# Four self attentions: score blocks with two heads on the rows and two batches on the columns, without block-diagonal squares, and with the row scale applied to the products

## What is computed

```python
q = jnp.einsum('bsc,hcd->bhsd', xn, wq)
k = jnp.einsum('btc,hcd->bhtd', yn, wk)
v = jnp.einsum('btc,hcd->bhtd', yn, wv)
a = jax.nn.softmax(jnp.einsum('bhsd,bhtd->bhst', q, k) * D ** (-0.5), axis=-1)
if causal:
    a = a * mask
o = jnp.einsum('bhst,bhtd->bhsd', a, v)
```

| stage | sublayer | heads x depth | special |
|---|---|---|---|
| A | `l0_xattn`, part a1 | 16 x 32 | mask behind the softmax |
| B | `l0_attn` | 16 x 16 padded to 32, in 8 pairs | the second head of a pair is subtracted, weighted by lambda |
| C | `l3_attn` | 16 x 64 | the output overwrites `V` |
| D | `l3_ffn` | 8 x 32 | |

## Time and profile before

### The profile page before, as it was taken

How to read it: one execution, slowest core, us unless ns; L and a number is a source line. 1 busy time by engine, 2 the same in 40 slices (tenths; PEclk the granted TensorE clock), 3 DMA queues, 4 the chain that set the end, 5 groups by cost and what they waited for, 6 DMA issues and landing times. The chain is left out here.

```text
span 5024.1 us, 105344 instructions
## 1 busy us (share of the span) xinstructions
PE 4240.7 (84%) x42698; PEld 3189.1 (63%) x42698; DVE 2661.6 (53%) x5277; ACT 1804.4 (36%) x3793; POOL 712.2 (14%) x422
## 2 busy tenths in 40 slices
PE   5869999999874969999976679586899899997877
PEld 3649888889554856666632369442699666665465
DVE  5447777777245026555539822246333566664544
ACT  1225555555211324444523312120344344443111
POOL 0013222222001010000009610115122000001100
PEclk8789999999975989999988879798799999999985
DMA  1110000000011841111003268549111100000211
GB/s 59 38 32 17 17 17 20 21 17 1 30 49 63 317 152 46 51 42 42 16 25 86 70 265 302 205 146 119 51 43 40 34 22 22 29 16 36 70 42 34
DMA packets 185482, 339.59 MB, mean 68 GB/s; under 512 B 53379, under 2 KB 136660, under 8 KB 167156
## 3 DMA queue, kind: packets, MB, share of 16 engines
q1 hardware_dynamic: 175348, 318.88, 20.3%
q0 software_dynamic: 3072, 8.39, 0.5%
q10 hardware_dynamic: 6624, 6.03, 0.3%
HBM read 278.31 MB, written 31.60 MB: 62 GB/s over the span
## 5 line engine op out<-in xcount | busy, mean ns | idle before, releaser
L2691 DVE TENSOR_REDUCE block_max<-PS 128x1 f32<-128x512 f32 (+1 forms) x896 | 505.7, 627 | 299.8 <-PE PS L2551 299.0
L2640 ACT ACTIVATE probs_turned<-PS 128x512 f32<-128x512 f32 (+1 forms) x896 | 434.5, 571 | 562.4 <-PE PS L2572 562.3
L844 PE MATMUL PS<-context_turned,queries 128*128 128x512 f32 (+1 forms) x1536 | 362.3, 380 | 21.7 <-issue 17.0
L905 ACT CAST probs_turned<-PS 128x512 fp32r<-128x512 f32 (+1 forms) x512 | 232.2, 510 | 280.4 <-PE PS L856 280.4
L876 PE MATMUL PS<-probs_turned,context_part 128*128 128x256 f32 (+1 forms) x2496 | 330.7, 286 | 2.2 <-DVE weighted L953 2.2
L844 PEld LDWEIGHTS PS<-context_turned,queries 128*128 128x128 f32 x1536 | 274.3, 195 | 75.2 <-issue 20.5
L919 DVE TENSOR_TENSOR probs_turned<-PS,probs_turned 128x512 fp32r<-128x512 f32 (+1 forms) x512 | 276.6, 582 | 64.9 <-ACT probs_turned L905 62.9
L876 PEld LDWEIGHTS PS<-probs_turned,context_part 128*128 128x128 f32 (+1 forms) x2496 | 307.1, 189 | 2.4 <-DVE probs_turned L919 2.4
L2592 PEld LDWEIGHTS PS<-probs_turned,values 128*17 128x17 f32 x13312 | 191.5, 97 | 147.6 <-issue 120.9
L2551 PE MATMUL PS<-keys_turned,queries 32*128 32x512 f32 (+1 forms) x2048 | 241.2, 548 | 40.3 <-ACT probs_turned L2640 35.3
L911 ACT ACTIVATE probs<-PS,minus_max 128x1024 f32<-128x1024 f32 (+1 forms) x256 | 238.7, 933 | 81.8 <-DVE minus_max L964 80.7
(11 more groups left out here) (504 smaller groups left out, 7581.6 us busy)
## 6 DMA issues: line engine op xcount, KB each, us to landing
context_rows<-in_ctx SPq DMA_DIRECT2D x40, 768.0 KB
context_turned<-ctx_turned SPq DMA_DIRECT2D x32, 800.5 KB
routed_up<-in_L_ffn_W SPq DMA_DIRECT2D x23, 1024.0 KB, 7.6
routed_down<-in_L_ffn_W SPq DMA_DIRECT2D x23, 1024.0 KB, 5.0
routed_up<-in_L_ffn_wg_w SPq DMA_DIRECT2D x23, 1024.0 KB, 7.4
routed_second<-in_L_ffn_w_w SPq DMA_DIRECT2D x23, 1024.0 KB, 9.6
routed_down<-in_L_ffn_w_w SPq DMA_DIRECT2D x23, 1024.0 KB, 4.9
v_all<-v_turned SPq DMA_DIRECT2D x128, 128.0 KB, 20.4
```

Of the source, the lines that this page charges most:

```text
L844: last = nc.tensor.matmul(S[:, 512 * j:512 * j + cols], qs[a][:, v, p * P:(p + 1) * P], yT[b][:, v, 512 * j:512 * j + cols], start=(m == 0 ...
L2640: nc.scalar.activation(probs[0:kk, t % ring, i, 0:many].rearrange("p k c s -> p (k c s)"), PS[0:kk, bank_of("turned", t, i), 0:many * 2 * ...
L2691: nc.vector.tensor_reduce(part[:, b % 2, chunks[0]:chunks[-1] + 1, i, u // 2], bank, AX_X, ALU.max).then_inc(max_done.sem, 1)
```

## The change

`self_attention` is rewritten; nothing else in the program differs. What it does:

- TensorE and VectorE read `qT`, `kT` and `V` in place. The staging DMAs, their buffers and waits are gone.
- A score block holds two heads on the two halves of the rows (`x`) and the two batches on the columns (`y`). The number of score products is the same. Head group `g` now always goes to row half `g % 2` of the output, so that with `d = 32` four cells are in use, not eight.
- A 128-column block of `E` can be turned as it is, two heads by two batches: there are 8 transposes per tile in A, B and C and 4 in D. `squares`, its clearing and its two copies are gone.
- The products with V are 64 rows by 64 columns: 32 per tile in A, B and C, 16 in D, two records each. Batch `y` has its keys on rows `y*64` and its output on partitions `y*64`, so that two of the four 64 x 64 cells are in use. The order alternates between them, and between two banks.
- The probabilities are not scaled. The row sums go through four small products with halves of the identity (`sums`), and `take` multiplies the products with V by the reciprocals, in two instructions, one per bank. In B the addition of the two heads follows there.
- In A the mask is applied by GpSimd, in two halves, between the exponential and the transposes.
- `E`, the turned blocks and the row sums have two buffers, and the hardware loops are unrolled.

The core of the diff, left out where it only renames:

```diff
-                    for h in range(heads):
-                        g, k = h % groups, h // groups
-                        for b in range(2):
-                            last = nc.tensor.matmul(PS[b * SEQ:(b + 1) * SEQ, g, k * SEQ:(k + 1) * SEQ],
-                                                    qs[g * d:(g + 1) * d, u, k, b * SEQ:(b + 1) * SEQ],
-                                                    ks[g * d:(g + 1) * d, u, k, b * SEQ:(b + 1) * SEQ],
-                                                    start=True, stop=True)
+                    for j0 in range(0, pairs, groups):
+                        for turn in range(2):
+                            for y in range(2):
+                                for g in range(groups):
+                                    x = g % 2
+                                    j = j0 + (g // 2 + (groups // 2) * ((x + turn) % 2) if groups == 4 else (x + turn) % 2)
+                                    k = (2 * j + x) // groups
+                                    rows = slice(g * d, (g + 1) * d)
+                                    at = (j // groups) * P + y * SEQ
+                                    last = nc.tensor.matmul(PS[x * SEQ:(x + 1) * SEQ, j % groups, at:at + SEQ],
+                                                            qT[rows, k, tokens(i, y)], kT[rows, k, tokens(i, y)],
+                                                            start=True, stop=True)
...
-                    for pos in range(squares):
-                        h = head_of(pos)
-                        last = nc.tensor.matmul(O_ps[:, h * dv:(h + 1) * dv], turned_sb[:, pos, :],
-                                                vs[:, u, h * dv:(h + 1) * dv], start=True, stop=True)
+                def sums(i):
+
+                    pe.wait_ge(summed.sem, summed.at(i + 1))
+                    if i:
+
+                        pe.wait_ge(o_taken.sem, o_taken.at(2 * i))
+                    for x, y in ((0, 0), (0, 1), (1, 0), (1, 1)):
+                        out = PS[y * SEQ:(y + 1) * SEQ, sum_bank + x, sum_col:sum_col + pairs].rearrange("p (g k) -> p g k", k=deep)
+                        last = nc.tensor.matmul(out, core.ident[:, x * SEQ:(x + 1) * SEQ], total[:, i % 2, :, :, y], start=True, stop=True)
+                    last.then_inc(moved.sem, 1)
...
+                def output(i, f):
+                    pe.wait_ge(t_act.sem, t_act.at(i * tfills + f + 1))
+                    for j0 in range(f * per_fill, (f + 1) * per_fill, 2):
+                        for turn in range(2):
+                            for x in range(2):
+                                for y in range(2):
+                                    j = j0 + (y + turn) % 2
+                                    rows = slice(y * SEQ, (y + 1) * SEQ)
+                                    at = (j // 2 * 2 + x) * dv
+                                    h = j if diff else 2 * j + x
+                                    last = nc.tensor.matmul(PS[rows, o_bank + j % 2, at:at + dv], ET[rows, i % 2, j, x * SEQ:(x + 1) * SEQ],
+                                                            V[rows, i, h * dv:(h + 1) * dv], start=True, stop=True)
...
-                    then(nc.vector.reciprocal(total[:], total[:]))
-                    if diff:
-                        odd = total[:, 1::2, :]
-                        then(nc.vector.tensor_scalar(odd, odd, minus_lam, None, ALU.mult))
-                    then(nc.vector.tensor_tensor(E[:], E[:], total[:].unsqueeze(3).broadcast_to([P, groups, per, SEQ]),
-                                                 ALU.mult))
-                    if mask is not None:
-                        Ef = E[:].rearrange("p g k t -> p (g k) t")
-                        then(nc.vector.tensor_tensor(Ef, Ef, mask[:].unsqueeze(1).broadcast_to([P, heads, SEQ]), ALU.mult))
...
+                    nc.vector.reciprocal(inverse[:, u].rearrange("p (k g x) -> p x g k", g=groups, x=2),
+                                         PS[:, sum_bank:sum_bank + 2, sum_col:sum_col + pairs].rearrange("p x (g k) -> p x g k", k=deep)
+                                         ).then_inc(inverted.sem, 1)
...
+                        nc.vector.tensor_tensor(by_bank(to), PS[:, o_bank + b, 0:pairs * dv].rearrange("p (q x n) -> p q x n", x=2, n=dv),
+                                                scale_of.unsqueeze(3).broadcast_to([P, pairs // 2, 2, dv]), ALU.mult).then_inc(o_taken.sem, 1)
...
+                        for k in range(deep):
+                            nc.gpsimd.tensor_tensor(kept[:, i % 2, :, k], E[:, i % 2, :, k],
+                                                    mask[:].unsqueeze(1).unsqueeze(1).broadcast_to([P, groups, 2, SEQ]),
+                                                    ALU.mult).then_inc(masked.sem, 1)
```

More of the change, by code:

```diff
@@ L425, in self_attention @@
     nc, PS = core.nc, core.PS
-    qc = qT.shape[1]
     groups = P // d
-    per = heads // groups
+    pairs = heads // 2
+    deep = pairs // groups
+    per_fill = 4
+    tfills = pairs // per_fill
     diff = minus_lam is not None
[L430 to L433, removed]
+    t_bank, o_bank = 4, 6
+    sum_bank, sum_col = (2, 0) if d == 64 else (o_bank, 448)
@@ L438, in self_attention @@
[L438 to L443, removed]
-    with ExitStack() as own:
[L446 to L453, removed]
+    o_ready, o_taken = core.semaphore("out_ready"), core.semaphore("out_taken")
@@ L454, in self_attention, with over_keys @@
         warm = core.sb(own, "warm", [1, 1])
[L455 to L458, removed]
+        S = PS[:, 0:groups, 0:deep * P].rearrange("p g (k y t) -> p g k y t", y=2, t=SEQ)
+        def over_keys(x):
+            return x.unsqueeze(4).broadcast_to([P, groups, deep, 2, SEQ])
         with nc.Block() as block:
[L460 to L480, removed]
@@ L502, in output @@
[L502 to L514, removed]
-                    for pos in range(squares):
-                        h = head_of(pos)
-                        last = nc.tensor.matmul(O_ps[:, h * dv:(h + 1) * dv], turned_sb[:, pos, :],
-                                                vs[:, u, h * dv:(h + 1) * dv], start=True, stop=True)
-                    last.then_inc(o_ready.sem, 1)
@@ new lines, in turn_exps @@
+                def turn_exps(i, f):
+                    n = i * tfills + f
+                    if mask is None:
+                        pe.wait_ge(exps.sem, exps.at(i + 1))
+                    else:
+                        pe.wait_ge(masked.sem, masked.at(i * deep + (f + 1) * deep // tfills))
+                    if n >= 2:
+                        pe.wait_ge(t_act.sem, t_act.at(n - 1))
+                    for m in range(per_fill):
+                        j = f * per_fill + m
+                        last = nc.tensor.transpose(PS[:, t_bank + n % 2, m * P:(m + 1) * P],
+                                                   kept[:, i % 2, j % groups, j // groups].rearrange("p y t -> p (y t)"), core.ident[:])
+                    last.then_inc(turned.sem, 1)
@@ L532, in _ @@
+                scores(0)
+                for i in range(TILES):
+                    if i + 1 < TILES:
+                        scores(i + 1)
+                    for f in range(tfills):
+                        turn_exps(i, f)
+                    sums(i)
+                    for f in range(tfills):
+                        output(i, f)
             @block.vector
@@ L605, in self_attention @@
-    probs.passed(2 * TILES)
-    if d == 64:
-        begun.passed(TILES)
+    o_taken.passed(2 * TILES)
     turned.passed(tfills * TILES)
-    t_act.passed(tfills * TILES + 2)
-    step.passed(steps * TILES + 1)
+    t_act.passed(tfills * TILES)
+    if diff:
+        signed.passed(TILES)
+        scaled.passed(TILES)
+    if mask is not None:
+        masked.passed(deep * TILES)
 def start_stores(core, block, pairs):
```

118 lines of the change are left out of this document (60 added, 58 removed).

## The result

The changed kernel takes 4917.8 us, the median of four runs (4907.3 to 4925.0 us). The ratio to the kernel before is 0.9773, with a 95% interval of 0.9751 to 0.9796: faster by 2.3%. The ratio leaves out the slow run of 7532.17 us among the runs of the kernel before. The profiled execution took 4912.93 us, 4911.1 us of them the span; before they were 5025.88 and 5024.1 us, so 113 us are gone. The forecast was 110. The number was met, but in part by two errors that cancel, and with another engine setting the pace in three of the four stages than the forecast had; both are taken up behind the experiments.

The account below looks back on a forecast made before the run. TensorE and VectorE were taken to wait for each other, neither full. Stage gains of 41 + 15 + 33 + 23 = 112 us, less 2 for shape changes, took 5025.9 to 4916 us; range 4885 to 4940.

Parts of the forecast that it names:

- The forecast that was preferred: Stages A to D: TensorE's tile at mostly the slow clock sets the pace; 4900 to 4928 us, chance 0.58.
- VectorE's tile: VectorE's work per tile after the change: 6.1 us in A, 6.8 in B, 6.6 in C, 3.7 in D.
- The products with V: Two-cell products at 55 ns a record at 1.2 GHz: 3.5 us a tile, 1.8 us in D.
- TensorE's slow tile: TensorE's work per tile at 1.2 GHz: 7.5 us in A, B and C, 4.6 us in D.
- the step on shape changes: TensorE changing array shape: 0.11 us a gap, two more in 32 tiles, 7 us if none hidden; 2 us carried.
- C's scores: C keeps its scores over four cells: 64 loads in 1.80 us at the slow clock, 1.02 us at the fast.
- The clock: TensorE's clock: B and D slow, C about half way, A a little fast; gains 41, 15, 33, 23 us in A to D.
- The mask: GpSimd's mask in A, two instructions of 1.27 us: costed at nothing, at most 20 us over eight tiles without cover.
- Start of a stage: Each stage loses the staging at its start, 3.5 us in A; scores come within 0.5 us of the block's start.
- The fast clock everywhere: Rival: TensorE at the fast clock in all stages, VectorE setting the pace; gain 141 us, 4885 us, chance 0.16.
- Pair without overlap: Rival: two cells do not fully overlap, or hidden dependencies show; 107 ns a record without overlap, up to 5014 us, chance 0.22.
- 216 ns a record: Rival: quarter products with V cost what the square ones do; 185 us slower, 5211 us, chance 0.04.

Follow-up runs that it names:

- e6: Changed kernel with VectorE taking the previous tile's products before the present tile's row sum; profiled span 4888.4 us, against 4911.1 and 4926.9 us for the changed kernel.
- e1: Changed kernel with all products with V of one batch before the other's within each group of four blocks; profiled span 4956.5 us, against 4911.1 us.

## Why the prediction was right, and where it was not

- **The sum.** Forecast 4916 us, measured 4917.8. The stages gave 127 and not 110; the tail gave back 11.7, which the forecast did not have. The nearness is in part two errors that cancel, and so in part luck.
- **What sets the pace.** The forecast that was preferred has TensorE's tile at mostly the slow clock. That holds in D alone. In B, in C and in A's tiles at 2.4 GHz VectorE's chain sets the pace (6.54, 6.22 and 5.69 us a tile), which the text had as its case for the fast clock.
- **VectorE's tile** was forecast at 6.1, 6.8 and 6.6 us in A, B and C and is 5.69, 6.54 and 6.22, since the two multiplications take 1.29 us together in C and 0.76 in A and B (1.38 and 0.85 in the forecast), the reciprocal starts 0.08 to 0.09 us ahead of the end of the row sum, and in A and C the row maximum starts as much ahead of the end of the multiplications; the term was sized up to 0.4 us too long. This is why B and C are 58.6 and 58.1 us, as the estimate at 2.4 GHz had them (58 and 57): they are bound by VectorE's chain, and B does not move between clocks of 0.73 and 0.76. In e6, with that chain shorter, both fall.
- **The products with V** at 55 ns a record at 1.2 GHz: 54.5. The estimate from four cells and from two column halves held. Scores in A and B (1.80 forecast, 1.79 measured) and D's distance between score groups (4.6; 4.70) held as well; the row sums were sized too short (0.4; 0.51).
- **TensorE's slow tile** was put at 7.5 us and is 7.9. The missing part is mostly the step on shape changes: 2 us were carried for all stages together, from the gap of 0.11 us of the earlier trace rows. The gap between scores and transposes is that size (0.12 us), that between transposes and row sums is 0.33 us at the slow clock and 0.17 at the fast, and between row sums and products 0.02 to 0.03. The profile puts none of these gaps down to a wait. What makes the one ahead of the row sums longer was not run apart.
- **C's scores: wrong.** The text said that C keeps its scores over four cells. The new order ties the row half of the output to the head group, and with two groups only two cells are left. The 64 loads take nearly twice what the earlier trace rows shows, as the timeline of C says:

```profile
4664.49 3.43 PEld L472 LDWEIGHTS PS<-kT,qT 64*64 64x64 f32 x64 [2.71 <-DVE exps L536]
```

```profile
4689.36 1.94 PEld L472 LDWEIGHTS PS<-kT,qT 64*64 64x64 f32 x64
```

  It cost nothing here, as C ran at 0.94 of full speed and VectorE's tile is the longer one: at 2.4 GHz the loads and gaps of a tile are 1.94 + 0.12 + 0.86 + 0.17 + 0.31 + 1.94 + some 0.1 = 5.4 us (an estimate from the rows of A and C) against 6.22. At 1.2 GHz the same sum, with the durations of the slow rows above, is 9.5 us, of which the two missing cells are 1.64, 13 us over the stage.
- **The clock.** D at 0.50 was right. B was forecast slow and ran at 0.73, C half way and ran at 0.94, A a little fast and ran at 0.73. This is the term that missed most, 7 us in B, 6 in A and 3 in C, all to the good side. The step that failed is the one that keeps B slow because B and D both have products of 32 columns and eight transposes. D and B now have the same forms and different clocks; what decides between them is open.
- **The mask** was costed at nothing. TensorE does idle for it, for 3.9 us over A by the groups, and the stage is 2 us shorter without it, though not in its tiles at 2.4 GHz. The forecast's own sign ("if TensorE idles for GpSimd's mask in A") came true, at a tenth of its bound.
- **Start of a stage: right.** Before, the scores started 3.5 us behind the block's first instruction. In the changed kernel they start with it, as the timeline of A says:

```profile
88.55 1.28 ACT L593 ACT_TABLE_LOAD   x1 [17.11 <-PEq L372]
88.55 1.05 PEld L472 LDWEIGHTS PS<-kT,qT 32*64 32x64 f32 x64 [1.85 <-issue]
```

- **The rivals.** The fast clock everywhere: no, D did not have it. Pair without overlap: e1 made something like it, and it cost 50 us, not the 93 of the text: a record is 89 ns and not 107, and where the clock is fast VectorE's tile covers most of it (C grew by 1.7 us). 216 ns a record: excluded by the 54.5.

## To carry to other kernels

When products use part of the array, order neighbours so that they do not share a cell: here alternating between two diagonal cells is worth 1.6 times on them (30 ns a record against 51 at 2.4 GHz), the alternation of banks included. Pairs that differ in the rows alone or in the columns alone were not run. Before counting on cells that a layout keeps, write down the (row, column) of each product in the new order; C lost half its cells that way, and its 64 loads of scores take 1.94 us in place of 1.02. Compare the stages that were edited and the one behind them, not totals, and look for a wait on another engine that the last tile's work could fill (in e6 a tile of C fell from 6.22 to 5.24 us).

## What the runs showed of the hardware

- TensorE was busy for 94% of D with four extra transposes a tile, at a granted clock of 0.50 throughout, while B, busy for 81%, got 0.73.
- The same code ran in the tail with the clock up for 17 us in both profiles of the kernel before (34.0 and 33.9 us) and for 3 to 4 us or not at all in twelve profiles of edited ones (43.7 to 45.7 us). A rise in the tail goes with a fast stretch that ended 22 us ahead of D, in 14 profiles; the cause is open.
- Products over two diagonal 64 x 64 cells: 54.5 and 30 ns a record at 1.2 and 2.4 GHz; in one cell in a row, with the bank alternating half as often, 89 and 51 ns (97 at 1.2 GHz in D).
- GpSimd's multiplication of 128 x 512 takes 1270 ns and that of 128 x 256 takes 726, so by these two, as an estimate, 182 ns of each do not scale with the width.
